# A macaron layer on one core: window loads issued from SyncE, values in two steps a group, eight turned slots

## The reference

```
x = x + 0.5 * ffn(layernorm(x))      # 8 experts, summed: (silu(x@wg) * (x@wu)) @ wd, inner width 512
x = x + attn(layernorm(x))           # 16 heads of 8 channels
x = x + 0.5 * ffn(layernorm(x))      # the same weights
```

```
scores = q k^T + einsum('bhqd,qkd->bhqk', q, rel);  attn = softmax(causal(scores))
ctx    = attn v + einsum('bhqk,qkd->bhqd', attn, rel);  out = ctx @ w_o.T
```

## Time and profile before

| | us |
|---|---|
| runs before: median (lowest, highest) | 1380.63 (1379.69, 1382.48) |
| the profiled execution, own time | 1380.33 |
| its span, first to last instruction | 1378.3 |
| PE busy | 1340.1 (97%) |
| DVE busy | 1196.6 (87%) |
| ACT busy | 1103.6 (80%) |
| POOL busy | 1098.8 (80%) |
| mean granted clock of TensorE | 0.991 |

### The profile page before, as it was taken

How to read it: one execution, slowest core, us unless ns; L and a number is a source line. 1 busy time by engine, 2 the same in 40 slices (tenths; PEclk the granted TensorE clock), 3 DMA queues, 4 the chain that set the end, 5 groups by cost and what they waited for, 6 DMA issues and landing times. The chain is left out here.

```text
span 1378.3 us, 29321 instructions
## 1 busy us (share of the span) xinstructions
PE 1340.1 (97%) x8472; PEld 1073.3 (78%) x8472; DVE 1196.6 (87%) x2554; ACT 1103.6 (80%) x2642; POOL 1098.8 (80%) x1012
## 2 busy tenths in 40 slices
PE   8999888998999999999999999999999999999898
PEld 7788676876787788777887888778887788778686
DVE  6887888998998999989999899999989999888565
ACT  7656778887888888879888898878988888888454
POOL 7977777787788887788889888798887887778565
PEclk9999989999999999999999999999999999999999
DMA  6404779999999999999999999999999999998100
GB/s 196 145 1 142 142 173 200 178 197 179 175 189 182 191 186 176 211 163 189 179 167 215 180 190 179 176 209 185 175 178 169 205 183 183 167 184 147 36 1 8
DMA packets 719137, 225.07 MB, mean 163 GB/s; under 512 B 653056, under 2 KB 698496, under 8 KB 718976
## 3 DMA queue, kind: packets, MB, share of 16 engines
q1 hardware_dynamic: 562224, 180.84, 71.1%
q10 hardware_dynamic: 156752, 42.36, 17.4%
HBM read 60.95 MB, written 69.86 MB: 95 GB/s over the span
## 5 line engine op out<-in xcount | busy, mean ns | idle before, releaser
L1230 POOL TENSOR_TENSOR hid_lo<-hid,hid_hi 128x512 fp32r<-128x512 f32 x512 | 661.5, 1301 | 154.1 <-ACT hid_hi L931 147.9
L925 ACT ACTIVATE hid<-work 128x512 f32<-128x512 f32 x512 | 307.8, 602 | 120.2 <-PE work L728 97.9
L1078 DVE TENSOR_TENSOR hid<-hid,work 128x512 f32<-128x512 f32 x512 | 347.5, 681 | 58.5 <-PE work L728 54.1
L1072 DVE SCALAR_TENSOR_TENSOR hid<-hid,work 128x512 f32<-128x512 f32 x512 | 346.5, 680 | 48.1 <-ACT hid L925 47.6
L1245 POOL TENSOR_TENSOR probs<-exps,probs 128x512 f16<-128x512 f32 (+1 forms) x288 | 304.6, 1060 | 79.0 <-ACT probs L988 75.8
L931 ACT CAST hid_hi<-hid 128x512 fp32r<-128x512 f32 x512 | 317.6, 625 | 22.7 <-DVE hid L1078 20.7
L976 ACT ACTIVATE exps<-work,negmax_shifted 128x512 f32<-128x512 f32 (+2 forms) x320 | 193.4, 607 | 59.3 <-DVE negmax_shifted L1178 41.3
L1172 DVE TENSOR_REDUCE negmax<-work 128x1 f32<-128x384 f32 (+3 forms) x352 | 222.7, 636 | 2.7
L809 PE MATMUL acc<-hid_lo,wd 128*128 128x512 f32 x512 | 211.4, 414 | 2.6 <-POOL hid_lo L1230 2.3
L726 PE MATMUL work<-xt,wg 128*128 128x512 f32 x512 | 205.6, 401 | 3.7 <-DVE xt L1047 1.5
L804 PE MATMUL acc<-hid_hi,wd 128*128 128x512 f32 x512 | 206.6, 403 | 1.0 <-ACT hid_hi L931 0.6
(11 more groups left out here) (99 smaller groups left out, 1918.0 us busy)
## 6 DMA issues: line engine op xcount, KB each, us to landing
prob_window_scratch<-probs SPq DMA_DIRECT2D x384, 80.0 KB, 2.8
rel_win<-rel_window_scratch ACTq DMA_DIRECT2D x250, 96.0 KB, 3.4
q_scratch<-rope SPq DMA_DIRECT2D x16, 512.0 KB, 4.3
qq<-q_scratch ACTq DMA_DIRECT2D x32, 256.0 KB
k_scratch<-rope SPq DMA_DIRECT2D x16, 512.0 KB, 4.7
rel_window_scratch<-g_s SPq DMA_DIRECT2D x32, 256.0 KB, 3.2
k_pad<-k_scratch SPq DMA_DIRECT2D x128, 64.0 KB, 3.8
prob_window_scratch<-probs SPq DMA_DIRECT2D x32, 256.0 KB, 3.7
```

The lines of the kernel that those rows point to most:

```text
L925: act.activation(hid[:, arg % HB, :], work[bank_of["gate", arg]][:, :], ACT.Tanh, scale=0.5).then_inc(s_tanh, 1)
L1072: dve.scalar_tensor_tensor(out=hid[:, arg % HB, :], in0=hid[:, arg % HB, :], scalar=1.0, in1=work[bank_of["gate", arg]][:, :], op0=ALU.add ...
L1078: dve.tensor_tensor(hid[:, arg % HB, :], hid[:, arg % HB, :], work[bank_of["up", arg]][:, :], ALU.mult).then_inc(s_hid, 1)
L1230: pool.tensor_tensor(hid_lo[:, arg % HH, :], hid[:, arg % HB, :], hid_hi[:, arg % HH, :].bitcast(F32), ALU.subtract).then_inc(s_hlo, 1)
```

## The change

- `load_window` moves from ScalarE's program to SyncE's, with its waits and both DMAs, and in the planner from the engine ACT to SP.
- `STAGES` becomes ((0, 1, 2), (3,)): two values steps a group, of 48 and 32 matmuls. `values_of` follows.
- TB becomes 8.
- The buffer `v_s` goes; v is made in the half `LO` of `rope`. So `v_add` waits until k's store has landed, and the first `rotate` of the next batch waits for the last `v_split`. The planner's conditions for `project`, `project_v` and `v_add` follow.
- All the shifts in `LATER` are new, and with them the order (the diff shows the first line of each).
- `dynamic_dma_scratch_size` goes from 1024 to 256.

```
--- before.py
+++ after.py
@@ -38,7 +38,7 @@
     XB = 5
     WB = 3
     VB = 3
-    TB = 6
+    TB = 8
     PB = 4
     EB = 2
 
@@ -82,12 +82,12 @@
         return k % GK in (2, 3, 4, 5, 6, 7, 8, 9, 10)
 
 
-    STAGES = ((0, 1), (2,), (3,))
+    STAGES = ((0, 1, 2), (3,))
     VG = len(STAGES)
     BANDS = ((0, 1, 2), (3,))
 
     def values_of(quad):
-        return quad // NT * VG + max(0, quad % NT - 1)
+        return quad // NT * VG + (0, 0, 0, 1)[quad % NT]
 
     def band_of(quad):
         return quad // NT * len(BANDS) + (0, 0, 0, 1)[quad % NT]
@@ -104,17 +104,17 @@
 
 
 
-    LATER = {"acc": -347.2, "attention_sum": -1143.5, "band_turn": -471.9, "band_values": -366.1, "constants":
...
+    LATER = {"acc": -794.3, "attention_sum": -333.6, "band_turn": -565.9, "band_values": -17.8, "constants":
...
 
     def step(engine, takes, time, name, arg, *after, lands=None):
         before = ()
@@ -218,10 +218,11 @@
             at = end + 12 + 8 * (w // 2)
             step("PE", 0.683, at, "project", (t, w), ("ln_lo", ("ln2", t)),
                  *([("project", (t, w - 1)), ("rotate", (t, w - 1))] if w else []),
-                 *([("qk_store", (t, 0))] if w == 2 else []), *([("qk_store", (t - 1, 1))] if w == 0 and t else []))
+                 *([("qk_store", (t, 0))] if w == 2 else []),
+                 *([("v_split", SPLITS * t - 1)] if w == 0 and t else []))
             step("DVE", wide(L) + w % 2 * 0.9, at, "rotate", (t, w), ("project", (t, w)))
-        step("PE", 1.33, end + 24, "project_v", t, ("ln_lo", ("ln2", t)))
-        step("DVE", wide(L), end + 24, "v_add", t, ("project_v", t), ("v_split", SPLITS * t - 1 if t else None))
+        step("PE", 1.33, end + 24, "project_v", t, ("ln_lo", ("ln2", t)), ("qk_store", (t, 1)))
+        step("DVE", wide(L), end + 24, "v_add", t, ("project_v", t), ("qk_store", (t, 1)))
         for i in range(SPLITS):
             step("POOL", (0.57, 1.12)[i % 2], end + 26 + 3 * i, "v_split", SPLITS * t + i, ("v_add", t),
                  ("values", VG * HG * (t - 1) - 1 if t >= 2 else None))
@@ -247,7 +248,7 @@
             for i in range(NT):
                 quad = NT * gg + i
                 begin = due[first_of(quad)]
-                step("ACT", 1.03, max(begin - 13, first - 13), "load_window", quad, ("qrel_store", gg),
+                step("SP", 1.03, max(begin - 13, first - 13), "load_window", quad, ("qrel_store", gg),
                      ("prepare_lo", 5), ("near", last_of(quad - WB) if quad >= WB else None), lands=LATE)
             for u, tiles in enumerate(BANDS):
                 last = NT * gg + tiles[-1]
@@ -408,9 +409,9 @@
         cos_s = sb("cos_s", [P, L])
         sin_s = sb("sin_s", [P, L])
         rope = sb("rope", [P, 2, L])
+        v_s = rope[:, LO, :].rearrange("p (a d) -> p a d", d=DH)
         qq = sb("qq", [P, 2, L], F32R)
         k_pad = sb("k_pad", [P, 2, HQ, L], F32R)
-        v_s = sb("v_s", [P, NT * H, DH])
         values = sb("values", [P, 2, NT, HQ, HG, VS, DH], BF16)
         rel_win = sb("rel_win", [P, WB, W, HQ])
         g_s = sb("g_s", [P, NT, R * HQ])
@@ -703,6 +704,22 @@
                         sp.dma_start(k_pad[R * a:R * (a + 1), arg % 2, a, :].bitcast(F32),
                                      bass.AP(k_t, t % VB * 4 * P * L + g * L + a * HG * L,
                                              [[H * L, 4 * DH], [1, L]])).then_inc(s_kld[arg % 2], 16)
+                if name == "load_window":
+                    gg, i = arg // NT, arg % NT
+                    sp.wait_ge(s_gst, 16 * (gg + 1))
+                    if arg >= WB:
+                        sp.wait_ge(s_near, last_of(arg - WB) + 1)
+                    elif arg < 2:
+                        sp.wait_ge(s_att_lo, 1)
+                        sp.wait_ge(s_relp, RELP)
+
+
+                    halves = ((0, P, 0, W),) if arg < WB else ((0, P // 2, 0, P // 2 + R), (P // 2, P, P // 2, W))
+                    for top, end, left, right in halves:
+                        sp.dma_start(rel_win[top:end, arg % WB, left:right, :].rearrange("p c a -> p (c a)"),
+                                      bass.AP(zwin_t, gg % 2 * NQ * TILE + i * HQ * W + top * NQ * W + left * HQ,
+                                              [[NQ * W, end - top], [1, (right - left) * HQ]])
+                                      ).then_inc(s_win[arg % WB], 16)
                 if name == "band_turn":
                     for u in range(len(BANDS)):
                         sp.wait_ge(s_bl[u], 16 * (arg + 1))
@@ -996,22 +1013,6 @@
                     act.dma_start(qq[:, arg % 2, :].bitcast(F32),
                                  bass.AP(q_t, t % VB * 4 * P * L + g * L,
                                          [[HG * L, HQ], [H * L, 4 * DH], [1, L]])).then_inc(s_qld[arg % 2], 16)
-                if name == "load_window":
-                    gg, i = arg // NT, arg % NT
-                    act.wait_ge(s_gst, 16 * (gg + 1))
-                    if arg >= WB:
-                        act.wait_ge(s_near, last_of(arg - WB) + 1)
-                    elif arg < 2:
-                        act.wait_ge(s_att_lo, 1)
-                        act.wait_ge(s_relp, RELP)
-
-
-                    halves = ((0, P, 0, W),) if arg < WB else ((0, P // 2, 0, P // 2 + R), (P // 2, P, P // 2, W))
-                    for top, end, left, right in halves:
-                        act.dma_start(rel_win[top:end, arg % WB, left:right, :].rearrange("p c a -> p (c a)"),
-                                      bass.AP(zwin_t, gg % 2 * NQ * TILE + i * HQ * W + top * NQ * W + left * HQ,
-                                              [[NQ * W, end - top], [1, (right - left) * HQ]])
-                                      ).then_inc(s_win[arg % WB], 16)
                 if name == "load_band":
                     gg, tiles = arg // len(BANDS), BANDS[arg % len(BANDS)]
                     top, n = NT * gg + tiles[0], len(tiles)
@@ -1135,7 +1136,7 @@
                     if w == 2:
                         dve.wait_ge(s_qst[0], 32 * (t + 1))
                     if w == 0:
-                        wait(dve, s_qst[1], 32 * t)
+                        wait(dve, s_vs, SPLITS * t)
                     dve.wait_ge(s_proj, 4 * t + w + 1)
                     dve.scalar_tensor_tensor(out=rope[:, (LO, HI)[w % 2], :], in0=work[bank_of["project", arg]][:, :],
                                              scalar=(QSCALE, 1.0)[w // 2], in1=(cos_s, sin_s)[w % 2][:, :],
@@ -1150,7 +1151,7 @@
                                                  op0=ALU.add, op1=ALU.add).then_inc(s_rope, 1)
                 if name == "v_add":
                     dve.wait_ge(s_projv, arg + 1)
-                    wait(dve, s_vs, SPLITS * arg)
+                    dve.wait_ge(s_qst[1], 32 * (arg + 1))
                     dve.tensor_tensor(v_s[:, :, :].rearrange("p (j h) d -> p j (h d)", j=NT),
                                       work[bank_of["project_v", arg]][:, :].rearrange("p (a b) -> p a b", a=NT),
                                       rel_v0[:, None, :].to_broadcast([P, NT, P]), ALU.add).then_inc(s_v, 1)
@@ -1324,7 +1325,7 @@
         "cos": np.repeat(cos, H, axis=0).astype(f32), "sin": np.repeat(sin, H, axis=0).astype(f32),
         "window": window.astype(f32), "ident": np.eye(P, dtype=f32), "lanes": lanes.astype(f32),
     }
-    nc = bacc.Bacc("TRN2", target_bir_lowering=False, num_devices=1, dynamic_dma_scratch_size=1024)
+    nc = bacc.Bacc("TRN2", target_bir_lowering=False, num_devices=1, dynamic_dma_scratch_size=256)
     given, args = {}, []
     for name, a in arrays.items():
         a = np.ascontiguousarray(a)
```

More of the change, by code:

```diff
@@ L103, in macaron_kernel @@
     LANDS = {"PE": 0.35, "ACT": 0.35, "DVE": 0.35, "POOL": 0.35, "SP": 2.6}
[L107 to L117, removed]
@@ new lines, in macaron_kernel @@
+    LATER = {"acc": -794.3, "attention_sum": -333.6, "band_turn": -565.9, "band_values": -17.8, "constants":
+             -193.0, "down": 6.9, "down_lo": -66.1, "exp": 23.1, "fill": 1516.0, "gate": -2.5, "gated": 159.6, "hi": 172.0,
+             "largest": -276.0, "ln_hi": 34.8, "ln_lo": -173.6, "ln_rstd": 220.6, "ln_scaled": -344.5, "ln_stats": -35.6,
+             "ln_turned": -186.8, "lo": 51.7, "load_band": -667.0, "load_expert": -1079.6, "load_k": 454.3, "load_q":
+             -741.4, "load_window": 441.5, "load_x": -556.0, "near": -228.0, "outproj": -139.3, "p_hi": -387.0, "p_lent":
+             -103.3, "p_lo": -377.8, "p_turn": 296.5, "prepare_hi": 39.2, "prepare_lo": 489.0, "product": 120.6, "project":
+             -306.2, "project_v": -480.7, "qk_hi": -686.9, "qk_lo": -914.6, "qk_store": -355.4, "qrel": 18.5, "qrel_copy":
+             -548.7, "qrel_store": -303.5, "recip": -1175.6, "recip_copy": -342.4, "recip_turned": 43.4, "recip_wide":
+             432.0, "rotate": 612.9, "scale": -215.6, "scores": 7.3, "shift": -316.3, "split_hi": 57.4, "split_lo": 471.0,
```

(2 more changed lines are left out.)

35 lines of the change are left out of this document (11 added, 24 removed).

## The result

The changed kernel took 1397.55 us (median of 4 runs, 1394.24 to 1399.44), beside 1380.89 for the kernel before on the same chip. The ratio is 1.0112, with a 95% interval of 1.0094 to 1.0130: 1.1% slower. The forecast was 1373.5, with a range up to 1396; the time is 1.6 us beyond its end and near the 1394 of rival (a).

What follows compares the result with a forecast made beforehand. TensorE's own work was taken as the bound. From 1380.3 us, -8.0 (values steps), -5.3 (window loads), +5.5 (slot waits) and +1 (v) gave 1373.5, 0.5% faster; range 1358 to 1396, the forecast's own 1365 to 1379.

Steps and rivals of the forecast that it cites:

- rival (a): Attention stretch, 142 to 1276: SyncE becomes the bound; 1394 us, sign TensorE's waits above 25 us; chance 0.25.
- Window loads from SyncE: Moving loads off ScalarE: -5.3 us, bounds -10.8 and 0; SyncE keeps 3.6 of 9.4 us free a group.
- +5.5: Price of SyncE's lost free time: TensorE's 5.5 us of named waits, 350 to 1290, double; bounds 0 and +54.
- Eight turned slots, waits: SyncE's transposes: task 8 waits for the merged values step, 2.3 us of delay a group; priced at +5.5 us.
- The slot wait: SyncE's waits for values, before task 8, up to some 20 or 30 cases.
- The block at 164: Window-load issue of 5.99 us on ScalarE; TensorE's 7.8 us hole plus lower clock behind it, 10.8 us, half saved.
- The merged step: Values in two steps instead of three, 32 groups: 0.25 us each, -8.0 us; between 3.8 and 9.9 saved.
- rival (c): Values steps: TensorE enters one step fewer but waits longer for the last transpose, cancelling; 1380 us, chance 0.17.
- v in the rope buffer: Next rope's wait for v's parts hidden, 0; VectorE's in-order wait for k's store +1 us, bounds 0 and +8.
- The new order: Same steps in other places, steady part and early part: 0 us, bounds -8 and +12.

Runs made afterwards that it cites:

- e5: Kernel before, order kept, windows still on ScalarE, with two small spare loads issued by SyncE at each window load's place: 1439.55 us, ratio 1.0433.
- e6: Changed kernel (windows on SyncE, merged step, eight slots, v in rope) with the shifts of the kernel before: 1413.09 us, ratio 1.0225.
- e7: Changed kernel with window loads planned and issued on ScalarE and the shifts of the kernel before: 1384.31 us, ratio 1.0032.
- e4: Kernel before with window loads planned and issued on SyncE, its shifts and three values steps kept: 1416.18 us, ratio 1.0252.
- e13: As e7 (windows on ScalarE, old shifts, eight slots, v in rope) but with three values steps a group: 1385.17 us, ratio 1.0030.
- e1: Kernel before, order kept, with only the window loads issued by SyncE at the same place: 1427.63 us, ratio 1.0345.
- e8: Changed kernel, order kept, second of each window's two loads left out from the fourth quad on: 1358.45 us, ratio 0.9842.
- e9: Control: kernel before, windows on ScalarE, second load of each window left out as well: 1373.45 us, ratio 0.9937.
- e10: Changed kernel, order kept, with the four key loads of each group issued by ScalarE instead of SyncE: 1460.30 us, ratio 1.0559.
- e2: Changed kernel with window loads issued by ScalarE at the same place of its own order: 1502.49 us, ratio 1.0882.
- e17: Repetition of e14, the changed kernel with paired band stores: 1380.58 us, ratio 0.9991.
- e11: Changed kernel, order kept, each window loaded in one DMA of all 160 columns instead of two of 96: 1393.47 us, ratio 1.0077.
- e18: Changed kernel with paired band stores and one load a window of all 160 columns together: 1383.47 us, ratio 1.0016.
- e15: Kernel before with tile 1's band stores in one DMA a task instead of two: 1379.08 us, ratio 0.9992.
- e14: Changed kernel, order kept, tile 1's band stores in one DMA a task instead of two, 64 issues fewer: 1377.79 us, ratio 0.9979.

## Why the prediction was wrong

The step that failed is the one on SyncE in "Window loads from SyncE" ("Of the 9.4 us free, 3.6 are left") and, resting on it, the **+5.5** of "Eight turned slots, waits". Point by point:

**SyncE's free time.** The 9.4 us a group came from summing the view of waits. The gaps of 0.3 us and more are 13.3% of 35.5, 4.7 us. The eight loads take the 5.8 I worked out. So the sum is 35.5 - 4.7 + 5.8 = 36.6 us a group; measured 36.2. That the sum comes so near is partly luck, for it isn't the whole price: by it the spare issues of e5, 8 x (0.59 + 0.1) = 5.5 us a group, would cost 0.8 a group, 26 us in all, and they cost 59, and one a window would be free and cost 10. Rival (a) had named the doubt, for another reason (the 0.1 us between issues; its "35.3 us" for the group should be 35.5), and I gave it 0.25. One addition of issue durations and gaps over a few groups of the timeline would have settled it before the forecast.

**The price of a fuller queue.** I took TensorE's 5.5 us of waits to double. They went to 26.0 from 350 to 1290, above the 25 that I had set as the mark for rival (a). The move measures +28.8 with the shifts kept (e6 less e7) and +35.3 in the structure before (e4); one and two spare issues a window cost 10 and 59. The late side was half foreseen: turns, yes; the windows themselves, whose place in the queue makes VectorE wait 36.7 us, no.

**The slot wait didn't come.** I expected 20 or 30 waits of task 8 for the merged step. The row is

```profile
SPq L689 <- PE ctx_p L890: 3.4, 2, 3.3
```

where before had 15.6 us in 14 cases, one of the twelve of the earlier trace rows. A queue that runs late finds the slot free. With the windows on ScalarE and SyncE free, the merged step does make the waits, in the number that I had set:

```profile
SPq L689 <- PE ctx_p L874: 24.0, 21, 3.3
```

(e7, whole span; e13, with three steps, has none.) And they cost nothing that can be told: e7 takes the time of e13. So the mechanism of my +5.5 was wrong, not only its size: the slot wait comes where the queue is free and costs nothing there, and where the queue is full it hardly comes and the price is paid without it.

**The block at 164 did go**, and the lower clock behind it. The stretch of the earlier trace rows in the windows view (busy of PE, PEld, DVE, ACT, POOL; granted clock):

```profile
176.00:182.00 6.00, 6.00 (x60) 4.99 (x59) 5.99 (x14) 4.91 (x12) 4.07 (x4) 1.00 1.05 177
321.00:326.00 5.00, 4.93 (x23) 3.59 (x21) 4.74 (x9) 4.66 (x13) 4.62 (x6) 1.00 1.03 182
```

60 matmuls where there were 18, and the second dip is gone too. The gain of 10.8 was not kept: the 67th turn starts at 360.3, where it started at 361.3 before, and TensorE waited 6.5 us for turns by 350. ScalarE's idle time ended by "issue" did not go near zero; four rows hold about 29 us, the longest single one 3.1.

**The merged step** is worth what I had set as the upper bound, but in TensorE's time only. A clean one:

```profile
640.61 0.85 PE L890 MATMUL ctx_p<-probs_t,values 128*24 128x128 f16 x48 [0.55 <-DMA probs_t<-probs]
641.38 0.50 PE L821 MATMUL acc<-hid_hi,wd 128*128 128x512 f32 x1
```

By distances of starts, steps of 24, 32 and 48 matmuls cost 0.648, 0.762 and 0.98 us all in, so two of 24 less one of 48 is 0.31 us, 10 us in 32 groups. With the windows on ScalarE, e13 (three steps) and e7 (two) take the same time. In their profiled executions TensorE's named waits from 350 to 1290 come to 7.9 us in e13 and 13.7 in e7, so some 6 of the 10 may have come back as waits, as rival (c) had it, though only 1.2 of them for turns. The rest isn't settled: each has an order of its own, and two orders of one structure differ by as much (e1 and e4: 11.4).

**v in the rope buffer** was not tried alone. With eight slots it costs 4.3 us (e13 less before), new order included; I had +1 and 0. VectorE's waits list none for `k_scratch`; the one for `q_scratch` is 2.9 us.

**The new order.** My 0 hides two things that I had not separated: the shifts give back 15.5 us of what the move costs, and would cost 28.6 without it. A hole grew behind the last output projection, where TensorE waits for a layernorm that goes from VectorE to GpSimd to ScalarE. It is 5.54 us, where before had 2.12 at 1302.78, and the granted clock behind it is 0.50, the lower level (1.2 GHz); before it fell there too (0.66 on average from 1300 to 1310):

```profile
1316.11 1.09 PE L749 MATMUL work<-ident,xn 128*128 128x128 f32 x4 [5.54 <-ACT xn L927]
...
1314.00:1324.00 10.00, 6.44 (x17) 4.94 (x18) 2.75 (x4) 3.42 (x7) 0.21 (x2) 0.50 0.00 0
```

In the forecast's own terms, with the runs' differences in their place: slots and v +4.3 (forecast +1), merged step -0.9 (-8.0), the move +28.8 (-5.3 + 5.5), shifts -15.5 (0), on 1380.9 (1380.3). That gives 1397.6. Of the 24.1 us of error the move makes 28.6, the merged step 7.1, slots and v 3.3, the base 0.6, and the shifts take 15.5 back. The terms depend on the order in which the parts are put in, and the small ones (slots and v, merged step) are no larger than the scatter between chips and orders. In the forecast +5.5 stood under the slots; here it is counted with the move, whose price it was to be.

The Trainium skill, DMA: Bandwidth & Descriptors, section "Issuing engines are not separate DMA queues", holds that spreading issues over engines only saves sequencer time, "which is usually small relative to the DMA itself". The first half agrees: both queues' packet time is 88.5% of the span before and 85.6% after (1220 and 1192 us), so the move changed little for the DMA engines. The second is true of one load here (0.59 us to issue, 4.3 to land) and misleads for the sum: sequencer time is what the 31 us of e8 beside e9 are. Its section "Queues, rings and completion order", that engines take turns between queue rows, led me to windows that land later. In the changed kernel they do (3.4 to 4.3 us), but where the move is alone they land sooner (2.8 in e1), so the runs don't bear this reading out.

## What to carry to other kernels

Before moving DMAs to a queue, add up that queue's issue durations and the short gaps between them over a few periods of the timeline; waits listed for a queue are not its free time. The price of an issue bends: here 0.08 us of the whole for each of the first 128, while 13% of real gaps shrank to 6%, and 0.38 for each of the next, and in the full queue two issues fewer a group brought 17 to 20 us. A searched order belongs to the engines it was searched for: compare structures only with each planned for itself, and expect some ten us of scatter from the order alone (e1 and e4: 11.4).

## What the runs showed of the hardware that was not expected

- Between two issues on SyncE that follow at once lies some 0.1 us. With 31 issues a group before and 39 after, these gaps are 5.9 and 7.1% of the queue, besides those inside rows of x2 and x4.
- An issue on ScalarE's queue directly behind band loads, or the q load and them, can take up to 6.16 us (e10; 5.87 in the timeline above), or 9.76 (e2), where the same load takes 0.4 to 0.6 in the middle. In the two places shown ScalarE starts no arithmetic meanwhile for 6 us (6.28 in the earlier trace rows, 6.31 in e10). What fills up there wasn't tried.
- Some kernels with a full SyncE scatter more from run to run: e17 from 1372.0 to 1387.7 (12 runs), e11 by 20.6 us and e18 by 19.3, where e15 goes from 1376.4 to 1382.7 (11 runs). It is no rule: e14, full too, spans 8.7 us, and e13, with a free SyncE, 10.
